# Second attention of a four-layer block: one list of four units per engine, and probability transposes in 64-row half tiles

## The chip, the cores and the metric

One core of a Trainium2 chip. The metric is device time in microseconds (us) of one execution, the median of the runs shown. In this text PE is TensorE, DVE VectorE, ACT ScalarE, POOL GpSimd and SP SyncE. PEld is PE's weight load, which may run beside its matmuls.

## The reference

All in f32, on x of 8 x 512 tokens of width 128; four layers, each behind a layer norm and added to x:

```
x = x + L0_attn(ln(x))     # 16 heads of 8, two softmaxes, difference with a learned lambda
x = x + L0_ffn(ln(x))      # 8 experts, top 2, capacity 1280, rows sorted into lists
x = x + L1_attn(ln(x))     # the change is here
x = x + L1_ffn(ln(x))      # 8 experts, top 4, and a shared expert

# L1_attn, b = 8 batches, 16 heads of 64, 512 tokens
K, Q, V = einsum('bpd,ihd->biph', x, W_K / W_Q / W_V)
scores  = einsum('biph,biqh->biqp', K, Q), causal mask
attn    = softmax(scores / 8)
z       = einsum('biph,biqp->biqh', V, attn)
out     = einsum('bqf,df->bqd', z as (b, q, 1024), W_O)
```

## The kernel before

Five instruction streams, one for each engine, are written by hand from one list, `schedule()`, and meet at semaphores (`Signal`). Every engine executes its own stream strictly in that order.

The second attention works on pairs of heads: 8 batches x 8 head pairs. A head pair has four *units*, one for each block of 128 query rows, in the order qb = 3, 0, 2, 1. A unit's scores are 128 x 128(qb+1), since the mask cuts the rest, so the four units have 512, 128, 384 and 256 columns. For a unit `u`:

- `scores1` (PE, L1391): two matmuls, one for each head of the pair, in the two 64-row tiles of the array (the head width is 64).
- `soft` (DVE, L2257): mask, scale and row maximum of each head, out of the PSUM pair `pS`.
- `exp1` (ACT, L1651): exp with the sum, for each head.
- `norm`: reciprocal (DVE, L2266) and multiplication (POOL, L2535).
- `turnp` (PE, L1404): transposes of the probabilities, 128 x 128 blocks, full array, head 0 into `tbank[0]`, head 1 into `tbank[1]`. ACT copies head 0 out (L1661), DVE head 1 (L2273).
- `values` (PE, L1424): once for a head pair, V times the transposed probabilities, both heads in two 64-column tiles, into `bank[2]`; ACT copies it out (L1669).

Beside them stand `heads` (H0 the queries, L1376 into `misc`, copied out by DVE, L2248; H1 the keys, L1372 into `bank[2]`, copied out by ACT, L1641), the value projection of the next batch (`v1`, L1361, into `misc` from the second batch on), the output projection once a batch (`op1`, L1433), transposes of the normed rows (L1165), router logits (L1269) and the combine of the expert rows (POOL fetches, DVE L2223, L2226). `misc` is one PSUM bank with many users; each waits until the one before has been copied out (`misc_free`).

The order of the second attention is the table `ROUND`. A round is two units, and a table row has two strings for each engine: rounds with an even and with an odd number. A token is a piece: S scores, M soft, X exp, N norm, T transposes (unit, head), H heads, V values, C a piece of the combine, A and B work of other stages, I the first value projections. `-1` says: of the round before. I call two rounds, four units, a *round pair*.

## Time and profile before

| | |
|---|---|
| median of 3 runs | 1513.7 us (1513.47 to 1518.37) |
| profiled execution, its own time | 1500.44 us |
| its span, first to last instruction | 1499.2 us |
| PE busy | 1437.6 us (96%) |
| DVE busy | 1074.6 us (72%) |
| ACT busy | 951.5 us (63%) |
| POOL busy | 745.5 us (50%) |
| mean granted clock of PE | 0.994 |

Busy time is what the profiler sees of an engine's instructions. A busy PE is not PE at its peak: drains and loads between matmuls are inside it, since the recorded ends of matmuls overlap. The profiled execution is one of its own, 13 us under the median of the timed runs.

### The profile page before, as it was taken

The page shows a single profiled execution, that of the slowest core. Times are in us where ns is not written, and L with a number is a line of the kernel's source. Part 1 is how long each engine was busy: PE and PEld are TensorE (multiplying, and loading weights), DVE is VectorE, ACT ScalarE, POOL GpSimd, SP SyncE. Part 2 cuts the span into 40 slices and gives each one's busy share as a digit, 9 for nine tenths or more (in the row PEclk, how much of TensorE's full clock was granted, in tenths as well). Part 3 has the DMA queues.
Part 4 walks back from the last instruction along what each step waited for, and adds up shares of the span by engine and source line. Part 5 has one row for each costly group of instructions (what it writes and reads, how often), then busy time and mean ns, then how long its engine had stood idle before and what let it go on. Part 6 is the DMA issues. An engine that isn't in the chain of part 4 may idle for free.

```text
span 1499.2 us, 26266 instructions
## 1 busy us (share of the span) xinstructions
PE 1437.6 (96%) x8801; PEld 856.5 (57%) x8801; DVE 1074.6 (72%) x3430; ACT 951.5 (63%) x2448; POOL 745.5 (50%) x1260
## 2 busy tenths in 40 slices
PE   4999999999989999979999999999999999998999
PEld 2434443444438889855565655656565565655666
DVE  5899999999944777547677687777767777674333
ACT  4588888887884334436767677676767777673221
POOL 7334656665455633633636365454636444353322
PEclk9999999999999999989999999999999999999999
DMA  7266655556334665720000000000000000020421
GB/s 142 57 159 134 143 141 148 110 106 150 113 131 165 213 211 190 256 64 1 15 1 15 1 12 5 3 14 1 16 2 14 3 1 2 2 58 1 99 76 52
DMA packets 70600, 113.39 MB, mean 76 GB/s; under 512 B 18857, under 2 KB 35114, under 8 KB 70458
## 3 DMA queue, kind: packets, MB, share of 16 engines
q0 software_dynamic: 33104, 61.73, 16.9%
q1 hardware_dynamic: 36928, 49.19, 10.9%
q8 instruction: 71, 1.16, 0.3%
q10 hardware_dynamic: 434, 0.79, 0.2%
q14 instruction: 63, 0.52, 0.1%
HBM read 71.86 MB, written 39.91 MB: 75 GB/s over the span
## 4 chain that ended last, share of the span: by engine, by line
PE 79%; DVE 10%; ACT 6%; issue 2%; POOL 1%; DMA 1%; SPq 0%; ACTq 0%; DVEq 0%; POOLq 0%
PE pS L1391 10%; PE bank L1424 9%; PE bank L1404 8%; PE bank L1235 6%; PE pS L1206 4%; PE bank L1433 4%; PE pS L1310 4%; PE bank L1376 4%; PE bank L1324 4%; PE bank L1361 4%; PE pS L1311 4%; PE bank L1372 3%; DVE mx L1831 3%; ACT ar L1561 3%; PE bank L1472 3%; PE bank L1226 2%
## 5 line engine op out<-in xcount | busy, mean ns | idle before, releaser
L2535 POOL TENSOR_SCALAR ar<-ar,rd 128x512 f32<-128x512 f32 (+3 forms) x512 | 269.3, 540 | 325.9 <-DVE rd L2266 324.0
L1831 DVE TENSOR_REDUCE mx<-pS 128x1 f32<-128x512 f32 x512 | 326.3, 677 | 19.4 <-PE pS L1206 17.6
L1651 ACT ACTIVATE ar<-ar,nm 128x512 f32<-128x512 f32 (+3 forms) x512 | 285.9, 560 | 83.1 <-DVE nm L2257 82.4
L2257 DVE CUSTOM_DVE_ANT_0 ar<-pS,maskf 128x512 f32<-128x512 f32 (+3 forms) x512 | 227.3, 481 | 6.3 <-PE pS L1391 4.4
L1561 ACT ACTIVATE ar<-bank 128x512 f32<-128x512 f32 x342 | 194.1, 598 | 44.8 <-PE bank L1226 41.6
L1404 PE MATMUL bank<-identr,all_r 128*128 128x128 f32 x1280 | 211.4, 287 | 4.6 <-DVE ar L2273 2.5
L1206 PE MATMUL pS<-all_r 64*128 64x512 f32 x512 | 205.7, 477 | 5.6 <-DVE mx L1831 4.7
L1404 PEld LDWEIGHTS bank<-identr,all_r 128*128 128x128 f32 x1280 | 134.3, 140 | 108.1 <-issue 83.4
L1661 ACT COPY ar<-bank 128x512 f32<-128x512 f32 (+3 forms) x256 | 107.4, 419 | 110.3 <-PE bank L1404 108.2
L1391 PE MATMUL pS<-ar 64*128 64x512 f32 (+3 forms) x1024 | 172.9, 456 | 0.8 <-DVE ar L2248 0.8
L1206 PEld LDWEIGHTS pS<-all_r 64*128 64x128 f32 x512 | 85.3, 192 | 127.7 <-DVE mx L1831 110.3
L2273 DVE COPY ar<-bank 128x512 f32<-128x512 f32 (+3 forms) x256 | 124.0, 484 | 40.9 <-PE bank L1404 39.8
L1424 PE MATMUL bank<-ar 128*64 128x512 f32 (+3 forms) x1024 | 152.0, 439 | 0.6 <-ACT ar L1661 0.6
L1226 PE MATMUL bank<-all_r 64*128 64x512 f32 x342 | 142.9, 458 | 1.8 <-ACT ar L1561 1.3
L1235 PE MATMUL bank<-ar 128*32 128x512 f32 x1024 | 139.8, 608 | 0.0
L1391 PEld LDWEIGHTS pS<-ar 64*128 64x128 f32 x1024 | 88.0, 186 | 68.8 <-issue 42.3
L1561 ACT ACTIVATE ar<-pS 128x512 f32<-128x512 f32 x170 | 101.6, 598 | 19.5 <-PE pS L1226 18.1
L2120 DVE TENSOR_TENSOR ar<-pS,ar 128x256 f32<-128x256 f32 (+1 forms) x156 | 59.2, 396 | 73.8 <-ACT ar L1600 73.5
L1424 PEld LDWEIGHTS bank<-ar 128*64 128x64 f32 x1024 | 67.9, 136 | 73.8 <-issue 59.1
L1600 ACT ACTIVATE ar<-pS 128x256 f32<-128x256 f32 (+1 forms) x156 | 56.8, 365 | 68.2 <-PE pS L1311 67.6
L1651 ACT ACTIVATION_READ_ACCUMULATOR ar<-ar,nm 128x1 f32 x512 | 97.0, 190 | 0.0
L2436 POOL DMA_DIRECT2D all_r<-dm x64 | 39.9, 627 | 95.0 <-DMA dm<-xT 90.1
(306 smaller groups left out, 2638.2 us busy)
## 6 DMA issues: line engine op xcount, KB each, us to landing
rows_in<-zrow SPq DMA_DIRECT2D x16, 1024.0 KB, 5.3
ar<-gd SPq DMA_DIRECT2D x16, 512.0 KB, 6.7
all_r<-dk POOLq DMA_DIRECT2D x56, 128.0 KB, 3.7
dk<-xT SPq DMA_DIRECT2D x21, 256.0 KB, 3.6
dq<-xT SPq DMA_DIRECT2D x16, 256.0 KB, 5.0
rows_out<-ar SPq DMA_DIRECT2D x32, 128.0 KB
all_r<-dq POOLq DMA_DIRECT2D x28, 144.0 KB, 3.8
all_r<-dq POOLq DMA_DIRECT2D x28, 128.0 KB, 3.4
```

The lines of the kernel that those rows point to most:

```text
L1206: M.matmul(bS[n % 3], qst[b % 2][rows, i, 128 * qb:128 * qb + 128], kst[b % 2][rows, i, :], start=True, stop=True).then_inc(*s_sc.inc(Gr, c))
L1226: M.matmul(bST[n % 3], kst[b % 2][rows, i, 128 * kb:128 * kb + 128], qst[b % 2][rows, i, :], start=True, stop=True).then_inc(*s_st.inc(Gr, ...
L1235: M.matmul(bO[32 * j:32 * j + 32, :], vst[b % 2][:, kb, 4 * g + j, :], pt[s_pv.no[Gr, kb, j] % NPT], start=(kb == 0), stop=(kb == 3)).then ...
L1391: M.matmul(pS[s][:, 512 * a:512 * a + w], yT[i][0][head, 128 * qb:128 * qb + 128], yT[i][1][head, 0:w], start=True, stop=True).then_inc(*s ...
L1404: ins = M.transpose(tbank[a][:, at_:at_ + 128].bitcast(F32R), pr_r[pi][:, 128 * t:128 * t + 128], identr[:, :])
L1424: ins = M.matmul(bank[2][64 * a:64 * a + 64, 128 * kb:512], v1[b % 2][:, kb, 64 * h:64 * h + 64], w, start=(kb == 0), stop=(kb == 3))
L1561: S.activation(pt[n % NPT], bST[n % 3], ACT.Exp, scale=QK_SCALE).then_inc(*s_ex.inc(Gr, kb, j))
L1651: S.activation(p, p, ACT.Exp, bias=nm1[:, c:c + 1], scale=-1.0, accum_out=den1[:, c:c + 1]).then_inc(*s_e1.inc(u, a))
L1831: V.tensor_reduce(mx[Gr % 2][:, col:col + 1], bS[n % 3], AX.X, ALU.max, negate=True).then_inc(*s_mx.inc(Gr, c))
L2257: V.tensor_tensor_reduce(pr_[pi][:, 0:w], pS[u % 2][:, 512 * a:512 * a + w], maskf[:, 512 - w:512], -0.125, 3e38, ALU.add, ALU.min, accum_ ...
L2273: V.tensor_copy(pT4[i][:, 3 - qb:4, w:w + 128], tbank[1][:, 0:w].rearrange("p (t n) -> p t n", n=128)).then_inc(*s_td.inc(u, 1))
L2535: G.tensor_scalar(p, p, rd1[:, c + a:c + a + 1], 1.0, ALU.mult, ALU.mult).then_inc(*s_p1.inc(u, a))
```

## The change

The rounds of two units become one list of four units for each engine (`PAIR`), whose loop runs over head pairs `z`. The keys `B0`/`B1` and `A0`/`A1` are what stood in the two rounds' B and A, C0 to C3 their four C. In the values' token V-1 the number now counts head pairs.

A unit's transposes become one piece for both heads (PE does all at `T`, and nothing at the token's second half). Each 128 x 128 block is turned as two halves: rows 0 to 63 and rows 64 to 127 of the probabilities, each with the 64 x 64 part of the identity, in the two 64-row tiles, half 0 into `tbank[0]` and half 1 into `tbank[1]`. So a transposed half has 128 partitions and 64 columns. ACT copies half 0 of both heads, in two instructions, DVE half 1. The wait is for both heads' probabilities and for both copies of the unit before.

```diff
-ROUND = {
-    "PE": ("S0 S1 T00-1 H0 T01-1 H1 I B T10-1 T11-1",
-          "S0 S1 T00-1 T01-1 V-2 T11-1 T10-1 I B"),
...
+PAIR = {
+    "PE": "S0 S1 T2-1 H0 H1 I B0 T3-1 S2 S3 T0 V-1 B1 T1",
+    "DVE": "M0 C0 N3-1 T21-1 H0 C1 H1 N0 M1 I B0 T31-1 A0 N1 M2 T01 C2 M3 N2 A1 C3 T11 B1",
...
+    for z in range(NU // 4 + 2):
...
+        pieces = {"I": taken(first_v1) if z == 0 else []}
         for n in range(2):
+            pieces["B%d" % n] = taken(beside_round, 2 * (z % 8) + n, b) if now else []
+            pieces["A%d" % n] = taken(after_round, 2 * (z % 8) + n, b) if now else []
+        for n in range(4):
             pieces["C%d" % n] = taken(next, back, None) if now else []
...
+    def turned_half(u, head, half):
+
+        qb, i = UNITS[u][2], (u // 4) % 2
+        n, w = 64 * (qb + 1), 128 * (qb + 1) + 64 * half
+        of_ = tbank[half][:, 256 * head:256 * head + n].rearrange("p (t n) -> p t n", n=64)
+        if head:
+            return pT4[i][:, 3 - qb:4, w:w + 64], of_
+        rows = pT[i][:, 128 * qb:128 * qb + 512 * (qb + 1)].rearrange("p (t n) -> p t n", n=512)
+        return rows[:, :, 64 * half:64 * half + 64], of_
...
         def turnp(u, a):
+
+            if a:
+                return
             qb = UNITS[u][2]
-            pi = (2 * u + a) % NP
-            PE.wait_ge(*s_p1.at(u, a))
+            PE.wait_ge(*s_p1.at(u, 1))
             if u:
-                PE.wait_ge(*(s_td if a else s_ta).at(u - 1, a))
-            else:
-                PE.wait_ge(*s_eo.at(NP_ - 2 + a))
+                PE.wait_ge(*s_ta.at(u - 1, 0))
+                PE.wait_ge(*s_td.at(u - 1, 1))
+            else:
+                PE.wait_ge(*s_eo.at(NP_ - 1))
             for t in range(qb + 1):
-                at_ = 128 * (qb - t if a else t)
-                ins = M.transpose(tbank[a][:, at_:at_ + 128].bitcast(F32R), pr_r[pi][:, 128 * t:128 * t + 128],
-                                  identr[:, :])
-            ins.then_inc(*s_t1.inc(u, a))
+                for head in range(2):
+                    to = 256 * head + 64 * (qb - t if head else t)
+                    for half in range(2):
+                        rows = slice(64 * half, 64 * half + 64)
+                        ins = M.transpose(tbank[half][:, to:to + 64].bitcast(F32R),
+                                          pr_r[(2 * u + head) % NP][rows, 128 * t:128 * t + 128], identr[rows, rows])
+                        if t == qb and head:
+                            ins.then_inc(*s_t1.inc(u, half))
...
-            V.tensor_copy(pT4[i][:, 3 - qb:4, w:w + 128],
-                          tbank[1][:, 0:w].rearrange("p (t n) -> p t n", n=128)).then_inc(*s_td.inc(u, 1))
+            for head in range(2):
+                to, of_ = turned_half(u, head, 1)
+                ins = V.tensor_copy(to, of_)
+            ins.then_inc(*s_td.inc(u, 1))
```

ACT's copy changes as DVE's does. Three places of the order show what moves.

PE, from the scores of units 0 and 1 of a head pair, before: transposes (L1404) of the head pair before stand ahead of, between and behind the queries (L1376) and keys (L1372).

```order
L1404 MATMUL bank<-identr,all_r 128x128 x2
L1361 MATMUL bank<-wv,xnT 128x512
L1391 MATMUL pS<-ar 128x512 x2
L1391 MATMUL pS<-ar 128x128 x2
L1404 MATMUL bank<-identr,all_r 128x128 x3
L1376 MATMUL bank<-xnT,res 128x512
L1404 MATMUL bank<-identr,all_r 128x128 x3
L1372 MATMUL bank<-xnT,att 128x512
L1361 MATMUL bank<-wv,xnT 128x512
L1404 MATMUL bank<-identr,all_r 128x128 x4
L1391 MATMUL pS<-ar 128x384 x2
L1391 MATMUL pS<-ar 128x256 x2
```

The same place in the changed kernel, where the scores are L1393, the transposes L1412, the queries L1378, the keys L1374 and the value projection L1363:

```order
L1271 MATMUL bank<-rt,xT 128x8 x4
L1412 MATMUL bank<-identr,all_r 128x64 x4
L1393 MATMUL pS<-ar 128x512 x2
L1393 MATMUL pS<-ar 128x128 x2
L1412 MATMUL bank<-identr,all_r 128x64 x12
L1378 MATMUL bank<-xnT,oT 128x512
L1374 MATMUL bank<-xnT,att 128x512
L1363 MATMUL bank<-wv,xnT 128x512
L1412 MATMUL bank<-identr,all_r 128x64 x8
L1393 MATMUL pS<-ar 128x384 x2
L1393 MATMUL pS<-ar 128x256 x2
```

All transposes of a unit stand together, next to scores, and queries, keys and value projection follow each other. The x12 are 6 couples of halves.

PE, around the values (L1424, after the change L1433), before, in a round pair whose second B is a value projection:

```order
L1404 MATMUL bank<-identr,all_r 128x128 x8
L1424 MATMUL bank<-ar 64x512 x2
L1424 MATMUL bank<-ar 64x384 x2
L1424 MATMUL bank<-ar 64x256 x2
L1424 MATMUL bank<-ar 64x128 x2
L1404 MATMUL bank<-identr,all_r 128x128 x2
L1361 MATMUL bank<-wv,xnT 128x512
```

and after:

```order
L1412 MATMUL bank<-identr,all_r 128x64 x16
L1433 MATMUL bank<-ar 64x512 x2
L1433 MATMUL bank<-ar 64x384 x2
L1433 MATMUL bank<-ar 64x256 x2
L1433 MATMUL bank<-ar 64x128 x2
L1363 MATMUL bank<-wv,xnT 128x512
L1412 MATMUL bank<-identr,all_r 128x64 x4
```

The value projection moved ahead of unit 1's transposes, which now stand directly before the next scores.

DVE, where the next batch's norm is applied (L1772, after the change L1781), before: the reciprocal, the norm, the copy of unit 1's transposes, then the soft pieces (L2257) of the next scores, the queries' copy (L2248) and unit 2's transposes' copy (L2273):

```order
L2266 RECIPROCAL rd<-den 128x2
L1772 TENSOR_SCALAR xn<-x,ln_mv,ln_rs 128x128 x4
L2273 COPY ar<-bank 128x128
L2266 RECIPROCAL rd<-den 128x2
L2257 ISA ar,nm<-pS,maskf 128x512
L2257 ISA nm 128x1
L2257 ISA ar,nm<-pS,maskf 128x512
L2257 ISA nm 128x1
L2248 COPY ar<-bank 128x512
L2273 COPY ar<-bank 128x3x128
```

and after (soft is L2266, the copies of the transposes L2283, the queries' copy L2257):

```order
L2275 RECIPROCAL rd<-den 128x2
L1781 TENSOR_SCALAR xn<-x,ln_mv,ln_rs 128x128 x4
L2283 COPY ar<-bank 128x64 x2
L2266 ISA ar,nm<-pS,maskf 128x512
L2266 ISA nm 128x1
L2266 ISA ar,nm<-pS,maskf 128x512
L2266 ISA nm 128x1
L2275 RECIPROCAL rd<-den 128x2
L2283 COPY ar<-bank 128x3x64 x2
L2257 COPY ar<-bank 128x512
```

Unit 2's copies moved ahead of the queries' copy; unit 1's copy still stands behind the norm.

## Rows read from the trace of the kernel before

**Rows 1.** The page: part 1, busy time by engine.
```profile
PE 1437.6 (96%) x8801; PEld 856.5 (57%) x8801; DVE 1074.6 (72%) x3430; ACT 951.5 (63%) x2448; POOL 745.5 (50%) x1260
```

**Rows 2.** The scores' line L1391: duration in ns, first and last start in us.
```profile
L1391 PE MATMUL pS<-ar x1024: 269/481/693, 658.0 to 1344.7; 64*128 64x512 f32 x43, 64*128 64x128 f32 x43, 64*128 64x256 f32 x43, 64*128 64x384 f32 x42
```

**Rows 3.** One batch: stretch, its length, busy time of PE, PEld, DVE, ACT, POOL, clock.
```profile
852.51:938.39 85.88, 85.66 (x548) 51.73 (x547) 63.80 (x258) 60.59 (x184) 45.40 (x80) 1.00 0.03 8
```

**Rows 4.** Chain of waits through one round pair: start us, us, what.
```profile
904.11 1.28 PE pS L1391 x8
905.39 0.38 PE bank L1404 x3
905.77 0.93 PE bank L1376 x2
906.70 0.21 PE bank L1404 x3
...
907.84 0.86 PE bank L1361 x2
908.70 0.29 PE bank L1404 x4
...
910.27 0.81 PE bank L1404 x8
911.07 2.31 PE bank L1424 x16
913.38 0.30 PE bank L1404 x2
```

**Rows 5.** PE's weight loads: start us, us, what; x8 is first start to last end.
```profile
906.11 0.14 PEld L1404 LDWEIGHTS bank<-identr,all_r 128*128 128x128 f32 x1 [0.24 <-POOL ar L2535]
...
910.20 0.73 PEld L1404 LDWEIGHTS bank<-identr,all_r 128*128 128x128 f32 x8 [0.33 <-issue]
```

**Rows 6.** Timeline at a 32-column transpose of the first attention.
```profile
216.02 0.10 PEld L1214 LDWEIGHTS bank<-identr,mp 128*32 128x32 f32 x1 [0.37 <-issue]
216.02 0.24 PE L1214 MATMUL bank<-identr,mp 128*32 128x128 f32 x1
...
216.06 0.30 PEld L1278 LDWEIGHTS bank<-rr,ustrict 128*128 128x128 f32 x2
```

**Rows 7.** Timeline at the queries of a round pair.
```profile
905.61 1.09 PE L1376 MATMUL bank<-xnT,oT 128*128 128x512 f32 x2
...
906.74 0.69 DVE L2248 COPY ar<-bank 128x512 f32<-128x512 f32 x1 [0.23 <-PE bank L1376]
...
907.48 0.39 PEld L1361 LDWEIGHTS bank<-wv,xnT 128*128 128x128 f32 x2 [0.47 <-DVE ar L2248]
```

**Rows 8.** Waits in the second attention: us in total, times, longest.
```profile
PEld bank L1361 <- DVE ar L2248: 19.9, 42, 0.5
```

**Rows 9.** Timeline where the next batch's norm is applied.
```profile
864.36 1.67 DVE L1772 TENSOR_SCALAR xn<-x,ln_mv,ln_rs 128x128 f32<-128x128 f32 x4
...
864.57 1.35 PE L1391 MATMUL pS<-ar 64*128 64x512 f32 x8
...
865.95 0.28 DVE L2273 COPY ar<-bank 128x128 f32<-128x128 f32 x1
```

**Rows 10.** Copies of the transposes: shape, count, busy us, mean ns.
```profile
L2273 DVE COPY ar<-bank 128x512 f32<-128x512 f32 x63 | 43.3, 687 | 1.9 <-PE bank L1404 1.8
...
L1661 ACT COPY ar<-bank 128x512 f32<-128x512 f32 x63 | 35.6, 565 | 0.0
...
L2273 DVE COPY ar<-bank 128x128 f32<-128x128 f32 x63 | 17.8, 283 | 18.9 <-PE bank L1404 18.4
L1661 ACT COPY ar<-bank 128x128 f32<-128x128 f32 x63 | 16.8, 266 | 25.3 <-PE bank L1404 24.8
```

**Rows 11.** DVE at the start of the second attention.
```profile
665.81 0.35 DVE L2223 SCALAR_TENSOR_TENSOR x<-ar,kw,x 128x128 f32<-128x128 f32 x1 [7.86 <-DMA ar<-rows_out,idx]
```

**Rows 12.** Chain of waits at the output projection: start us, us, what.
```profile
852.51 7.16 PE bank L1433 x64
```

More of the change, by code:

```diff
@@ L591, in schedule, with part @@
     back = returned(1)
-    def part(token, x, pieces):
+    def part(token, z, pieces):
         name, late = token.split("-") if "-" in token else (token, "0")
-        y = x - int(late)
+        y = z - int(late)
         kind, n = name[0], name[1:]
-        if kind in "CAI":
+        if kind in "ABCI":
             return pieces[name]
-        if kind in "BV":
-            z = (y - 1) // 2
-            if kind == "B":
-                return pieces["B"]
-            return [("values", (z, kb)) for kb in range(4)] if y % 2 and 0 <= z < NU // 4 else []
-        if not 0 <= y < NU // 2:
+        if not 0 <= y < NU // 4:
@@ L606, in part @@
             return []
-        u = 2 * y
+        u = 4 * y
+        if kind == "V":
+            return [("values", (y, kb)) for kb in range(4)]
         if kind == "H":
-            r = 8 * (y // 16) + y % 16 // 2 + 1
-            return [("heads", (r // 8, r % 8, int(n)))] if y % 2 == 0 and r < 8 * NB else []
-        if kind == "S":
-            return [("scores1", (u + int(n),))]
-        if kind == "M":
-            return [("soft", (u + int(n),))]
-        if kind == "N":
-            return [("norm", (u + int(n),))]
@@ L617, in part @@
-        return [({"X": "exp1", "T": "turnp"}[kind], (u + int(n[0]), int(n[1])))]
-    def first_v1(x):
-        for t in (2 * x, 2 * x + 1):
+            r = y + 1
+            return [("heads", (r // 8, r % 8, int(n)))] if r < 8 * NB else []
+        if kind == "T":
+            return [("turnp", (u + int(n[0]), int(n[1:] or 0)))]
+        if kind == "X":
+            return [("exp1", (u + int(n[0]), int(n[1])))]
+        return [({"S": "scores1", "M": "soft", "N": "norm"}[kind], (u + int(n),))]
@@ L621, in first_v1 @@
+    def first_v1():
+        for t in range(4):
             add("v1", 0, t, 0)
             add("v1", 0, t, 1)
-    for x in range(NU // 2 + 5):
-        b, k = x // 16, x % 16
-        now = x < NU // 2
-        if now and k == 8 and b + 2 < NB:
+    for z in range(NU // 4 + 2):
+        b = z // 8
+        now = z < NU // 4
+        if now and z % 8 == 4 and b + 2 < NB:
             back = returned(b + 2)
-        pieces = {"I": taken(first_v1, x) if x < 2 else [], "B": taken(beside_round, k, b) if now else []}
+        pieces = {"I": taken(first_v1) if z == 0 else []}
@@ L630, in schedule @@
         for n in range(2):
+            pieces["B%d" % n] = taken(beside_round, 2 * (z % 8) + n, b) if now else []
+            pieces["A%d" % n] = taken(after_round, 2 * (z % 8) + n, b) if now else []
+        for n in range(4):
             pieces["C%d" % n] = taken(next, back, None) if now else []
-        pieces["A"] = taken(after_round, k, b) if now else []
-        for engine, rounds in ROUND.items():
-            for token in rounds[x % 2].split():
-                for unit in part(token, x, pieces):
+        for engine, tokens in PAIR.items():
+            for token in tokens.split():
+                for unit in part(token, z, pieces):
@@ L928, in program @@
     s_p1 = Signal(nc, "probs1", [(u, a) for (u,) in of("norm") for a in range(2)])
-    s_t1 = Signal(nc, "probs_turned", of("turnp"))
+    s_t1 = Signal(nc, "probs_turned", s_s1.marks)
     s_ta = Signal(nc, "turned_by_act", [k for k in of("turnp") if k[1] == 0])
@@ L1656, in turnp @@
                 return
-            qb, i, w = UNITS[u][2], (u // 4) % 2, 128 * (UNITS[u][2] + 1)
             ACTE.wait_ge(*s_t1.at(u, 0))
-            o = pT[i][:, 128 * qb:128 * qb + 512 * (qb + 1)].rearrange("p (t n) -> p t n", n=512)
-            S.copy(o[:, :, 0:128],
-                   tbank[0][:, 0:w].rearrange("p (t n) -> p t n", n=128)).then_inc(*s_ta.inc(u, 0))
+            for head in range(2):
+                to, of_ = turned_half(u, head, 0)
+                ins = S.copy(to, of_)
+            ins.then_inc(*s_ta.inc(u, 0))
         def values(pair, kb):
@@ L2270, in turnp @@
                 return
-            qb, i, w = UNITS[u][2], (u // 4) % 2, 128 * (UNITS[u][2] + 1)
             DVE.wait_ge(*s_t1.at(u, 1))
-            V.tensor_copy(pT4[i][:, 3 - qb:4, w:w + 128],
-                          tbank[1][:, 0:w].rearrange("p (t n) -> p t n", n=128)).then_inc(*s_td.inc(u, 1))
+            for head in range(2):
+                to, of_ = turned_half(u, head, 1)
+                ins = V.tensor_copy(to, of_)
+            ins.then_inc(*s_td.inc(u, 1))
         def op1(b):
```

11 rows, old and new, of tables (PAIR, ROUND) are left out of this document.

## Prediction

> **What bounds the kernel now.** I read four views in this order. The page's first part [rows 1] says that PE is busy for 96% of the span, DVE for 72% and ACT for 63%, so the question is what the change does to PE's list. The second attention runs from the first L1391 matmul at 658.0 us to about 1355 us [rows 2]. The busy time in one batch of it, 85.88 us from one output projection to the next [rows 3], is 85.66 us for PE at full clock, 63.80 for DVE and 60.59 for ACT. The reader is to see that PE has no idle time to give here: only work or switches taken from PE shorten it. The chain of waits of one round pair [rows 4] confirms it, since every piece is PE's, one after another, with no wait between them. Eight batches of such pairs make the stretch.
>
> That chain prices every piece, because PE is in order (of pieces that come twice one row stands: the keys and a second value projection read 0.93 like the queries, the second scores 1.28). From [rows 4], in us: scores of two units 1.28; 3 transposes behind scores 0.38; queries (L1376) behind transposes 0.93; 3 transposes behind a projection 0.21; keys 0.93; a value projection (L1361) behind another projection 0.86; 4 transposes 0.29; scores 1.28; 8 transposes 0.81; values 2.31; 2 transposes 0.30. The sum is 9.58 us, and a second value projection adds 0.93.
>
> Three prices follow.
> - A transpose: (0.81 - 0.38)/5 = 0.086 us. The load row agrees: 8 loads in 0.73 us, one alone 0.14 long, so (0.73 - 0.14)/7 = 0.084 apart [rows 5].
> - A change of tile shape. A 512-column projection takes 0.86, so 640 columns of scores should take 1.07 and took 1.28: 0.21. Scores to transposes costs 0.38 - 0.21 = 0.17. The 1280 columns of values should take 2.15 and took 2.31: 0.16. Behind values, 2 transposes took 0.30 instead of 0.13: 0.17. So each change costs 0.16 to 0.21 us, the drain and a weight load that nothing hides.
> - A full-width f32 load behind a short matmul: 0.93 - 0.86 = 0.07.
>
> The Trainium skill (TensorEngine Tiling (Array Packing), Key Properties) says the same of the first part, that changing the tiling mode drains the engine; by that, the trace agrees.
>
> **The change, part by part.** Per round pair (four units) PE's list goes from six changes of shape to four (scores and transposes now share the 64-row shape), or five where a piece stands in B1, between values and the last transposes.
>
> *Transposes.* 20 full ones become 20 couples, two 64-row halves side by side. The moving operand halves to 64 columns, the stationary one keeps 128. What matters is whether the load or the matmul sets the 0.085. A load of 32 columns (L1214) is followed by the next instruction's load 0.04 later, although the matmul between them also moves 128 columns [rows 6]. So the pace follows the loaded columns and does not wait for a 128-column matmul. I take 0.085 a couple: no gain from the halves. That two row tiles load and stream side by side is shown by the scores: 8 matmuls, two heads in two row tiles, fit into the 1.28 that one head's columns explain. Bounds: 0.06 a couple if the pace was the matmul's, 0.17 if the tiles take turns.
>
> *The round pair without waits.* Scores behind a same-shape transpose 1.07 + 0.10 = 1.17; 6 couples 0.21 + 3 x 0.085 = 0.46, less 0.03 for the shorter last matmul; queries behind a change 1.06; keys 0.86; value projection 0.86; 4 couples behind a change 0.44; scores 1.17; 8 couples 0.61; values 2.31; 2 couples behind a change 0.27. Sum 9.18: 0.40 less. With a piece in B1 (six of eight pairs in a batch) a fifth change costs about 0.13 of that: 0.25 less. Per batch: 2 x 0.40 + 6 x 0.25 = 2.3 us.
>
> *A new wait behind the queries' copy.* Before, 3 transposes (0.21) stood between queries and keys. Now queries, keys and the piece in B0 follow each other, and the piece in B0 needs the same bank as the queries, emptied by DVE (L2248). In [rows 7] the queries' last matmul is recorded to end at 906.70, the copy runs from 906.74 to 907.43, PE's load starts at 907.48, and 0.10 of it is exposed: 1.05 after the queries leave the array at about 906.53. The keys cover 0.86, so at least 0.19 is bare. DVE also has the two score reductions, a reciprocal and now two transpose copies ahead of that copy, which makes it about 0.13 later. I take 0.32 for each of the seven pairs in eight whose B0 is filled: 2.2 us a batch. The list before paid next to nothing for it: the whole stretch has 19.9 us of "load waits for L2248", hidden behind the matmul then running [rows 8].
>
> *Coupled transposes wait for both copies.* Each unit's transposes now need both engines' copies of the unit before and both heads' probabilities. Where the next batch's norm is applied (L1772, 1.67 us on DVE [rows 9]), DVE's copy of the one-column-block unit ends 1.66 after the scores start (864.57 to 866.23). PE wants the next transposes at 1.08, so it stands 0.6 to 1.0: I take 0.8 a batch.
>
> *Copies.* 256 copies on each of ACT and DVE become 512 of half the width. From 266 to 565 ns on ACT and 283 to 687 on DVE over 128 to 512 columns [rows 10], a copy has a fixed part of 0.165 and 0.148 us. Extra per batch: 32 x 0.165 = 5.3 us on ACT (77% busy) and 4.7 on DVE (80%). Neighbours on DVE overlap by about 0.08 [rows 7], so what later work feels is about 0.07 a unit. It is hidden by PE's own time except where PE waits for the copy, which the two waits above include. If that cover is gone, it is 0.3 us a pair, 18 us in all.
>
> *The rest.* DVE's first reduction now stands ahead of the first combine, which waits 7.86 us for a DMA [rows 11]. The queries' copy still stands behind that combine, so this gives back 1 us at most. SP's list only renames its rounds, and POOL's tensor_scalars keep their number.
>
> Sum: 8 x (-2.3 + 2.2 + 0.8) = +5.6, less about 1 at the start: **+5 us**. The profiled execution took 1500.4 us (span 1499.2), the median of the three runs shown is 1513.7. I add the 5 us to the median: 1519. About 0.3% (4.5 us) is what this measurement can tell from no change.
>
> **The rivals.**
> - *The pace falls with the moving columns* (0.06 a couple). 20 x 0.025 x 64 = 32 us leave PE's work, but DVE and ACT, then at 82% and more, and the waits for copies give back about half: 5 - 15 = -10 us, 1504. The sign turns at 0.077 a couple. For it: the matmul and the load are both 128 wide in every L1404 row, so those rows can't tell them apart. Against it: [rows 6]. The Trainium skill (TensorE: Matmul & The Clock Gate, Part 3) has a rule that leads here, that a load overlaps running matmuls only when the row group differs; the value projection's load of 907.48, all rows, starts while the keys' matmuls still run, until about 907.84 [rows 4, 7], which speaks against it.
> - *Two row tiles are slower than one full array for this operation*: loads at the f32 pace (0.112 for 128 columns, 7.16 us for 64 [rows 12]), or tiles that take turns. At 0.11: 20 x 0.025 x 64 = +32, of which the new waits swallow about 15, so 5 + 17 = +22, 1536. The Trainium skill (TensorE: Matmul & The Clock Gate, LDWEIGHTS) gives 128/1.2 = 107 ns for any load of 128 columns; the L1404 loads here are 84 apart. At 0.17: 20 x 0.085 x 64 = +109, less some 30 of waits that it hides, 1593. For it: no transpose in a 64-row tile is in the trace. Against it: the scores run side by side.
> - *The copies become the path*: DVE's and ACT's lists slip, PE waits the 0.3 us a pair above on top: +5 + 15, 1534. For it: coupled releases, 80% busy in order. Against it: DVE still waits for PE, 0.23 ahead of the queries' copy [rows 7].
> - *Nothing shows*: the waits are 0.1 a pair smaller than walked and changes of shape are worth their full 0.2: within 4 us of before.
>
> **How the numbers follow.** Forecast (pace near 0.085, waits as walked, -1 to +11 us): 50%, of which about two fifths stay under 4.5. Moving columns: 18%, plus 3% for smaller waits that end faster too. Slower tiles: 12%, two thirds of it near +22. Copies: 12%. Nothing shows: 5%. Faster by over 0.3%: 0.21. Within: 0.2 from the forecast, 0.05, and 0.05 of the middle between rivals: 0.3. Slower: 0.49. The range from 1504 (first rival) to 1536 (0.11 a couple, or copies) leaves out the serial tiles and the far end of the first rival, some 15 to 20%.
>
> **What the changed profile would show.** Scores next to transposes with no gap, four couples' loads 0.085 apart, and a round pair of about 9.5 us without and 10.5 with a piece in B1. A new group of waits on PE, for DVE's queries' copy, of about 0.3 each some 50 times, and one for transposes after the norm's application. ACT and DVE near 77% and 80% a batch. The forecast is wrong if the couples' loads are not 0.08 to 0.09 apart, if PE's waits for copies come to less than 1.5 us or more than 5 us a batch, or if the scores behind transposes still cost 1.28.

## The result, and the profile after

The changed kernel takes 1521.3 us (median of 12 runs), the kernel before 1513.65 beside it (12 runs): ratio 1.0046, 95% interval 1.0025 to 1.0068. Two disturbed runs of the changed kernel are left out of the ratio. On another chip it was compared once more (below): 1.0033, 1.0005 to 1.0061. So it is slower by 5 to 7 us; the forecast was +5.

Batches are numbered from 0 here, and so are a batch's eight round pairs where they carry a number. "PE stands" means idle time of PE in the chain of waits.

The page of the changed kernel, part 1, for [rows 1]:

```profile
PE 1437.8 (95%) x10081; PEld 851.7 (56%) x10081; DVE 1082.6 (71%) x3686; ACT 962.5 (64%) x2704; POOL 745.0 (49%) x1260
```

PE's busy time has not moved (1437.6 before), DVE gained 8.0 us and ACT 11.0. The span of this execution, 1514.6 us, is not to be set against the 1499.2 of before: the first L1393 scores start at 667.2 us, 9.2 later than in [rows 2], although the program up to there is the same, and every execution profiled on one of the three chips used below has this lag (664.9 to 669.6), those on the other two have not (658.0 to 660.5). Which chips the first comparison and the profile of before ran on is not known. By the lag, the changed kernel's first profile is from the third chip and that of before is not; that would also explain why the profile of before (1500.44 us) lies 13 us under its timed median, since the kernel before has medians of 1502.35, 1503.03 and 1512.92 us on the three chips. So I compare stretches.

Two batches of the changed kernel, in the columns of [rows 3], batch 3 and batch 6 (the second window begins one pair into it):

```profile
934.69:1022.16 87.47, 85.34 (x710) 50.83 (x709) 64.95 (x288) 62.16 (x216) 45.30 (x81) 1.00 0.03 8
1206.47:1292.75 86.28, 85.33 (x711) 50.88 (x709) 62.75 (x282) 61.87 (x218) 37.42 (x73) 1.00 0.01 2
```

Before, each batch takes 85.88 us. Batch 6 here takes 86.28, batch 3 takes 87.47, with PE busy for 85.3 us in both, 0.3 less than before. PE's idle time grew from 0.2 us to 0.95 and 2.1. The two do not separate work from waiting: a matmul that waits for its weights is recorded longer, so the waits behind the keys below are inside the busy time.

The chain of waits of a round pair, for [rows 4], here one with a value projection in B1:

```profile
924.34 1.18 PE pS L1393 x8
925.52 0.43 PE bank L1412 x12
925.95 1.05 PE bank L1378 x2
927.01 0.86 PE bank L1374 x2
927.86 0.03 issue
927.89 1.12 PE bank L1363 x2
929.02 0.44 PE bank L1412 x8
929.46 1.18 PE pS L1393 x8
930.64 0.59 PE bank L1412 x16
931.23 2.30 PE bank L1433 x16
933.53 1.06 PE bank L1363 x2
934.59 0.27 PE bank L1412 x4
```

The reader is to see the forecast pieces: scores behind transposes 1.18 (1.17 forecast), 6 couples behind them 0.43, queries behind a change of shape 1.05, keys 0.86, 4 couples 0.44, 8 couples 0.59, values 2.30, 2 couples 0.27. From 6 to 8 couples is 0.16 us (0.59 less 0.43), so 0.08 a couple, the pace of before. All of these are within 0.03 of the forecast. Only the value projection behind the keys is long: 0.03 and 1.12 in place of 0.86.

Why it is long is in the timeline at the queries, for [rows 7]:

```profile
936.40 1.13 PE L1378 MATMUL bank<-xnT,res 128*128 128x512 f32 x2
...
937.15 0.60 DVE L2283 COPY ar<-bank 128x192 f32<-128x192 f32 x2
...
937.67 0.68 DVE L2257 COPY ar<-bank 128x512 f32<-128x512 f32 x1
...
938.41 0.30 PEld L1363 LDWEIGHTS bank<-wv,xnT 128*128 128x128 f32 x2 [0.86 <-DVE ar L2257]
```

DVE's copy of the queries (L2257) follows the copy of unit 2's transposes (L2283) without a gap, and PE's load for the value projection follows the queries' copy. The load's idle time of 0.86 is mostly covered by the keys' matmuls; what PE itself waits is 1.15 - 0.86 = 0.29 us (0.32 forecast).

Where the next batch's norm is applied, for [rows 9]:

```profile
872.40 1.35 PE L1393 MATMUL pS<-ar 64*128 64x512 f32 x8
872.46 1.69 DVE L1781 TENSOR_SCALAR xn<-x,ln_mv,ln_rs 128x128 f32<-128x128 f32 x4
...
874.07 0.34 DVE L2283 COPY ar<-bank 128x64 f32<-128x64 f32 x2
...
874.56 0.67 PE L1412 MATMUL bank<-identr,all_r 64*128 64x64 f32 x12 [0.81 <-DVE ar L2283]
```

PE could start the transposes of unit 2 at 873.5, 1.1 behind its scores, and does at 874.56, behind DVE's norm and the copy of unit 1: 1.06 us a batch (0.8 forecast).

The copies of the transposes by shape, for [rows 10] (count, busy us, mean ns):

```profile
L2283 DVE COPY ar<-bank 128x256 f32<-128x256 f32 x128 | 48.0, 417 | 0.8 <-PE bank L1412 0.8
...
L1670 ACT COPY ar<-bank 128x256 f32<-128x256 f32 x128 | 41.4, 375 | 56.4 <-PE bank L1412 56.4
...
L2283 DVE COPY ar<-bank 128x64 f32<-128x64 f32 x128 | 22.3, 215 | 32.6 <-PE bank L1412 32.2
...
L1670 ACT COPY ar<-bank 128x64 f32<-128x64 f32 x128 | 20.8, 214 | 37.6 <-PE bank L1412 37.1
```

Two half copies are busy 0.75 us on DVE (48.0/64) where one whole took 0.69, and 0.35 where it took 0.28: 0.06 more, not the fixed part of 0.148, because neighbours on an engine overlap.

**What the forecast did not have.** In one or two round pairs of each of five batches the wait behind the keys is 0.5 to 0.85 us longer. The timeline of pair 6 of batch 2:

```profile
913.95 0.68 PE L1412 MATMUL bank<-identr,all_r 64*128 64x64 f32 x12
...
915.93 0.62 DVE L2283 COPY ar<-bank 128x192 f32<-128x192 f32 x2 [0.53 <-PE bank L1412]
...
917.38 1.13 PE L1363 MATMUL bank<-wv,xnT 128*128 128x512 f32 x2 [0.83 <-DVE ar L2257]
```

The transposes of unit 2 run at 913.95. Their semaphore counts up at 915.87, 1.24 us after the end that the record gives, where outside these pairs it is 0.01 after it. (This pair is in batch 2; batch 3 has the same in its pairs 5 and 6.) DVE stands 0.53 us for it, copies, copies the queries, and PE stands 0.83. In batch 3 that makes 87.47 out of 86.28.

### The profile page after: what moved, and what is told of

Read it like the earlier page. It is cut to its first block, busy times and chain, and to the rows that moved or that the text cites. A ratio compares the mean times of both kernels' runs of the same rounds, so it can differ in the third digit from the quotient of the medians.

```text
span 1514.6 us, 29146 instructions
## 1 busy us (share of the span) xinstructions
PE 1437.8 (95%) x10081; PEld 851.7 (56%) x10081; DVE 1082.6 (71%) x3686; ACT 962.5 (64%) x2704; POOL 745.0 (49%) x1260
## 4 chain that ended last, share of the span: by engine, by line
PE 76%; DVE 12%; ACT 6%; issue 3%; POOL 2%; DMA 1%; ACTq 0%; DVEq 0%; POOLq 0%
PE pS L1393 8%; PE bank L1433 8%; PE bank L1412 7%; PE bank L1237 6%; PE bank L1363 4%; PE bank L1378 4%; PE pS L1208 4%; PE bank L1442 4%; DVE mx L1840 4%; PE pS L1312 3%; PE pS L1313 3%; PE bank L1326 3%; PE bank L1481 3%; PE bank L1374 3%; PE bank L1228 3%
## 5 line engine op out<-in xcount | busy, mean ns | idle before, releaser
L2266 DVE CUSTOM_DVE_ANT_0 ar<-pS,maskf 128x512 f32<-128x512 f32 (+3 forms) x512 | 227.6, 482 | 16.8 <-PE pS L1393 16.0
L1670 ACT COPY ar<-bank 128x256 f32<-128x256 f32 (+3 forms) x512 | 122.8, 292 | 152.1 <-PE bank L1412 151.5
L2283 DVE COPY ar<-bank 128x256 f32<-128x256 f32 (+3 forms) x512 | 140.1, 315 | 75.4 <-PE bank L1412 75.1
L1412 PEld LDWEIGHTS bank<-identr,all_r 64*128 64x128 f32 x2560 | 128.7, 137 | 81.2 <-POOL ar L2545 68.1
L1393 PE MATMUL pS<-ar 64*128 64x512 f32 (+3 forms) x1024 | 173.2, 457 | 0.8 <-DVE ar L2257 0.8
L1412 PE MATMUL bank<-identr,all_r 64*128 64x64 f32 x2560 | 157.4, 252 | 12.2 <-DVE ar L2283 7.2
L1433 PE MATMUL bank<-ar 128*64 128x512 f32 (+3 forms) x1024 | 152.5, 440 | 0.7 <-ACT ar L1670 0.7
L1393 PEld LDWEIGHTS pS<-ar 64*128 64x128 f32 x1024 | 87.7, 186 | 49.9 <-issue 31.2
L1433 PEld LDWEIGHTS bank<-ar 128*64 128x64 f32 x1024 | 68.2, 137 | 72.3 <-issue 59.4
```

The costliest lines, as they stand in the source:

```text
L1393: M.matmul(pS[s][:, 512 * a:512 * a + w], yT[i][0][head, 128 * qb:128 * qb + 128], yT[i][1][head, 0:w], start=True, stop=True).then_inc(*s ...
L1412: ins = M.transpose(tbank[half][:, to:to + 64].bitcast(F32R), pr_r[(2 * u + head) % NP][rows, 128 * t:128 * t + 128], identr[rows, rows])
L1433: ins = M.matmul(bank[2][64 * a:64 * a + 64, 128 * kb:512], v1[b % 2][:, kb, 64 * h:64 * h + 64], w, start=(kb == 0), stop=(kb == 3))
L2266: V.tensor_tensor_reduce(pr_[pi][:, 0:w], pS[u % 2][:, 512 * a:512 * a + w], maskf[:, 512 - w:512], -0.125, 3e38, ALU.add, ALU.min, accum_ ...
L2283: ins = V.tensor_copy(to, of_)
```

## The experiments

All times are ratios to the kernel before on the same chip, with the 95% interval. "A batch" is the length of batch 3, from its first scores to the next batch's. Three chips were used: e1 to e4 ran on one, e5 to e8 on a second, e9 to e12 on a third. The changed kernel itself was timed on the second (e8) and, by its lag, on the third, not on the first.

| run | ratio | interval | a batch, us |
|---|---|---|---|
| kernel before | 1 | | 85.9 |
| changed kernel | 1.0046 | 1.0025 to 1.0068 | 87.5 |
| e1 fetches apart | 0.9993 | 0.9967 to 1.0019 | 86.3 |
| e2 norm one pair later | 1.0143 | 1.0108 to 1.0177 | 91.2 |
| e3 queries' copy first | 1.0025 | 0.9997 to 1.0054 | 86.2 |
| e4 order alone | 1.0034 | 1.0009 to 1.0058 | 87.1 |
| e5 norm in the gap | 0.9976 | 0.9951 to 1.0001 | 85.5 |
| e6 e5 and e3 | 0.9972 | 0.9948 to 0.9997 | 85.2 |
| e7 e6, whole transposes | 1.0067 | 1.0044 to 1.0090 | 87.2 |
| e8 changed kernel again | 1.0033 | 1.0005 to 1.0061 | 86.3 |
| e9 ACT's copy early | 1.0057 | 1.0035 to 1.0079 | 87.6 |
| e10 filler in the last pair | 1.0036 | 1.0021 to 1.0050 | 87.5 |
| e11 e5, e9, e10 | 1.0012 | 0.9998 to 1.0027 | 86.8 |
| e12 e5, e10 | 1.0000 | 0.9981 to 1.0019 | 86.6 |

### The late signals: e1 and e8

```diff
-    "POOL": "N3-1 N0 C0 N1 A0 C1 N2 A1 C2 C3",
+    "POOL": "N3-1 C3 N0 C0 N1 A0 C1 N2 A1 C2",
```

> POOL's two row fetches that stand side by side behind the norm of unit 2 (C2 C3) are taken apart: C3 now stands behind the norm of unit 3. In the changed kernel the unit 2 transposes of two pairs in a batch (the sixth and seventh, batches with fetches alone) have their end signalled 1.1 to 1.2 us late, and PE then waits 0.5 and 0.75 us more behind the keys. Theory A, the late signal belongs to the fetches that run at that moment: the two waits go, about 1.25 us in each of five batches, -6 us against the changed kernel (ratio to before 1.0005 in place of 1.0046). Theory B, it belongs to the router pieces of these pairs, or to the half transposes as such: the late signals stay where they are and the time with them, 0. If the signal is late wherever a fetch meets a transpose, it may also move to another place: then between 0 and -6.

The late signals were gone and a batch took 86.3. That looked like theory A. The changed kernel itself, run again on the second chip, takes the conclusion away:

> The changed kernel itself once more, beside the others on this chip. If the late end signals of the transposes in the sixth and seventh pair belong to the program, they are there again, in the same five batches, and the batch takes 87.4 us; if they were an accident of one profiled execution, the batch takes 86.3. The ratio to before should be 1.003 to 1.006.

The same place, transposes of unit 2, their copy and the value projection behind the keys, in e8:

```profile
901.13 0.68 PE L1412 MATMUL bank<-identr,all_r 64*128 64x64 f32 x12
...
902.50 0.60 DVE L2283 COPY ar<-bank 128x192 f32<-128x192 f32 x2
...
903.75 0.30 PEld L1363 LDWEIGHTS bank<-wv,xnT 128*128 128x128 f32 x2 [0.85 <-DVE ar L2257]
```

The copy follows with nothing to wait for, although the fetches (POOL L2535) stand where they stood. Its batch:

```profile
1016.79:1103.06 86.27, 85.33 (x710) 50.90 (x708) 64.61 (x289) 61.90 (x218) 45.03 (x80) 1.00 0.03 8
```

So the late signals do not belong to the program alone, nor are they an accident of one execution, as they come back below. Neither of the two first chips showed one in any of eight profiles of seven different edits and the changed kernel; the third chip showed them in all four of its profiles, e9 to e12, and the changed kernel's first profile has them, with the 9 us lag of that chip. On that chip they stand in the six batches that have fetches (0 to 5) and in neither of the two that have none (batch 6 above, at 86.28, and the last). That the fetches take part is thus likely; that separating them helps was not shown, since e1 did not run there. Whether the kernel before has late signals there is open too. They cost the changed kernel about 1.2 us in four batches and 0.5 in one, some 5 us of that profile, but its ratio is only 0.0013 higher than e8's, inside the intervals. Nor is e1's 0.9993 a gain over e8's 1.0033: the intervals overlap, the chips differ, and the batches of both profiles are equally long to 0.1 us (86.33 and 86.27).

### The order alone: e4

```diff
             for t in range(qb + 1):
                 for head in range(2):
...
+                    ins = M.transpose(tbank[head][:, at_:at_ + 128].bitcast(F32R),
+                                      pr_r[(2 * u + head) % NP][:, 128 * t:128 * t + 128], identr[:, :])
...
```

Each engine's copy of a unit is one instruction again, as before.

> The new order of all engines, with both heads' transposes together, but the transposes as before: full array, 128 x 128, one copy for each engine. This separates the order from the half tiles. My theory: the half tiles save the changes of shape between scores and transposes, 0.40 us in a pair without and 0.25 in one with a piece in B1, 2.3 us a batch; without them the new order has before's changes and the new waits (queries' copy, norm, late signals), so +18 us against the changed kernel, about +25 against before, less some 3 us for waits that the longer list hides: ratio 1.013 to 1.017. Rival: half tiles bring nothing net because two copies per engine in place of one cost what the shapes save: then this kernel takes the time of the changed one, ratio about 1.005.

The theory's 1.013 to 1.017 failed: 1.0034, the time of the changed kernel (1.0033 on another chip), as its rival had it. But this batch is not the changed kernel's:

```profile
1011.93:1099.06 87.13, 86.83 (x547) 51.55 (x545) 63.44 (x256) 60.73 (x184) 45.03 (x81) 1.00 0.03 7
```

87.13 us: the order alone costs 1.25 a batch over before, and the half tiles then give back 0.85, not 2.3. PE has 86.83 us of work here, 1.5 more than with half tiles, but the longer list also covers waits: the value projection behind the keys takes 1.05 in place of 1.15, since one copy of unit 2 on DVE is 0.53 long and two are 0.60, and at the norm PE stands 0.36 us instead of 1.06. (Of the 1.5 us, the waits behind the keys count as busy in both.) Behind the output projection DVE has an unbroken list of 6.4 to 6.6 us up to the copy of unit 1, which PE must wait for; what PE saves in that pair it only waits longer. That the timed ratio is no higher in spite of the longer batches has a counterpart behind the stretch: e4's profile takes 159.7 us from the last pair's scores to its end, e8's 166.9 (below).

### The norm: e2 and e5

e2 moves the application one pair later, and with it all of A0, ahead of the copy of unit 3.

```diff
-        if k == 3 and b + 1 < NB:
+        if k == 4 and b + 1 < NB:
             add("apply", "c", b + 1)
-    "DVE": "... M1 I B0 T31-1 A0 N1 M2 ...",
+    "DVE": "... M1 I B0 A0 T31-1 N1 M2 ...",
```

> DVE applies the next batch's norm (1.69 us) one pair later and in another place of its list: ahead of the copy of unit 3's transposes, where it stands idle for 1.2 us, in place of ahead of unit 1's copy. My theory, that coupled transposes wait for the norm's application: PE's wait of 1.06 us behind the scores goes in seven batches, -7.4 us against the changed kernel, ratio about 0.9997. Rival: the work is only moved and DVE's list is what counts; then unit 3's copy, about 0.5 later, makes the transposes of unit 0 wait instead, and the gain is under 3 us.

It was 1.4% slower, so the rival held. The copy of unit 3 and the transposes of unit 0 in one of the three pairs that grew:

```profile
871.49 0.48 DVE L2283 COPY ar<-bank 128x128 f32<-128x128 f32 x2
...
872.12 1.03 PE L1412 MATMUL bank<-identr,all_r 64*128 64x64 f32 x16 [1.67 <-DVE ar L2283]
```

DVE's idle time ahead of that copy is not slack: PE wants unit 0's transposes right behind the next scores. They wait 1.67 us here, and the statistics and the router's pieces, which moved along, cost two more pairs 1.06 and 0.92. The wait is the same, 1.66 to 1.68 us, in batches 2 to 6, but what follows is not: in three of them (2, 3, 5) PE then has 3.4 us at the lower clock level and the pair is 2.7 us longer than in e8, in the other two (4, 6) the clock stays and the pair is 1.1 longer. The batch of 91.2 us in the table is one of the three; batches 4 and 6 take 89.5 and 89.4. The moved work must go where both DVE and what follows it wait for something long. That is the output projection:

```diff
-        if k == 2 and b + 1 < NB:
+        if k == 2 and b == 0:
             add("ln", "c", b + 1)
-        if k == 3 and b + 1 < NB:
+        if k == 3 and b == 0:
             add("apply", "c", b + 1)
...
+    def next_norm(b):
+        add("ln", "c", b + 1)
+        add("apply", "c", b + 1)
...
+        pieces["L"] = taken(next_norm, b) if z % 8 == 1 and 0 < b < NB - 1 else []
-    "DVE": "... N0 M1 I B0 T31-1 ...",
+    "DVE": "... N0 M1 I L B0 T31-1 ...",
-    "POOL": "N3-1 N0 C0 ...",
+    "POOL": "N3-1 N0 L C0 ...",
```

> The next batch's norm (statistics, root, application; 1.2 us and 1.7 us on DVE) moves to where DVE stands idle for 7.0 us behind the output projection, ahead of that wait, in the six batches that have an output projection. Nothing else changes against the changed kernel. My theory, DVE's unbroken list from the output projection to the copy of unit 1's transposes (6.6 us) is what PE waits for in the next scores: the wait of 1.06 us goes, 6 x 1.06 = -6 us against the changed kernel, and the six pairs from the output projection on read about 8.9 us in place of 9.9. Rival, drawn from the last run in which this norm was moved and cost 3 us or more a batch: any move of it delays a copy that PE needs; then not faster.

DVE around the output projection in e5, statistics, application and the addition of the projection:

```profile
851.90 0.87 DVE L1736 BATCH_NORM_STATS2 ln_st<-x 128x6 f32<-128x128 f32 x4
...
854.67 1.12 DVE L1786 TENSOR_SCALAR xn<-x,ln_mv,ln_rs 128x128 f32<-128x128 f32 x4 [1.49 <-POOL ln_rs L2391]
...
859.01 0.69 DVE L2294 TENSOR_TENSOR x<-bank,x 128x512 f32<-128x512 f32 x1 [3.22 <-PE bank L1447]
```

All of it lies ahead of the 3.22 us that DVE still waits. The batch is 85.48 us, 0.8 less than e8's, and the pair behind the projection 9.09 in place of 9.9 (8.9 was expected). The ratio is 0.9976, beside e8's 1.0033 on the same chip, where the intervals still overlap. The third chip has a second pair of kernels that differ in this move alone, e12 and e10 below: 1.0000 (up to 1.0019) against 1.0036 (from 1.0021), 0.36% or 5.4 us, where 6 were expected. These intervals do not overlap, so the norm's move is a gain that the timed runs show.

```profile
1009.22:1094.70 85.48, 85.08 (x709) 50.94 (x708) 64.24 (x288) 61.71 (x216) 44.99 (x81) 1.00 0.03 8
```

### The queries' copy: e3, e6 and e7

```diff
-    "DVE": "M0 C0 N3-1 T21-1 H0 C1 ...",
+    "DVE": "M0 C0 N3-1 H0 T21-1 C1 ...",
```

> DVE copies the queries ahead of unit 2's transposes. My theory: PE's wait behind the keys is the copy's own latency plus 0.10 us for which DVE is held by the other copy. The wait falls from 0.25-0.30 to 0.15-0.20, and in the two pairs with a late signal DVE no longer stands in front of it, so 7 x 0.10 + up to 0.5 = 0.7 to 1.2 us a batch, -6 to -9 us. Rival: DVE then stands idle for about 0.4 us ahead of the queries' copy in each pair, its list slips by as much, and unit 0's or unit 1's exponentials or copies come late: 0 or slower.

Each pair with a queries' wait became 0.10 us shorter (9.36 for 9.46, 10.41 for 10.51), as forecast, but a batch stayed at 86.2: in the pair behind the norm unit 2's copy came late for unit 3 (+0.5), and in the last batch, which has no value projections, five of the seven pairs lost 0.3 to 0.65 in this way (71.8 for 70.1 us over all seven). So theory and rival each held in their place.

> The norm in the gap and, on DVE, the queries' copy ahead of unit 2's transposes. If the waits are what ate the gain of the half tiles, a batch takes 86.25 (queries first) less 1.05 (norm) less 0.5 (the third pair, where unit 2's late copy held up unit 3) = 84.7 us against 85.87 before: 6 to 7 batches x 1.2 = -8 us against before, ratio 0.994 to 0.996. Rival, the two moves disturb each other as DVE is 80% busy: ratio 0.998 or more.

```profile
1009.38:1094.56 85.18, 84.63 (x710) 50.83 (x709) 65.09 (x288) 62.05 (x216) 45.01 (x81) 1.00 0.03 8
```

85.18 us, 0.7 under before, ratio 0.9972: the lowest ratio measured, but 0.0004 from e5, so no gain over it is shown. The forecast of the batch was 84.7, too low by 0.5, of which the pair behind the norm's old place kept 0.3 (9.38 for e5's 9.09); the last batch is 1.7 longer than e5's (71.8 for 70.1), as in e3.

> The same two moves with the transposes as before (full array, 128 x 128, one copy for each engine). It prices the half tiles with the waits largely gone. My theory: half tiles save 0.40 us in a pair without and 0.25 in a pair with a piece in B1, 2.3 us a batch, of which the first comparison showed only 0.84 because waits took the rest; here 1.6 to 2.3 us a batch show, this kernel is 13 to 18 us slower than the one with half tiles. Rival: the extra copies cost as much wherever they stand, and the difference stays at 0.84 a batch, 7 us.

```profile
1017.28:1104.53 87.25, 86.77 (x547) 51.53 (x545) 63.90 (x256) 61.29 (x184) 45.02 (x81) 1.00 0.03 7
```

With whole transposes the same two moves bring nothing (87.25 after 87.13). Against e6 this is 2.07 us a batch, and 0.95% = 14 us of the kernel: here the half tiles show what they save, inside both ranges of the theory. The chain of a pair of e7, beside that of the changed kernel above:

```profile
1006.74 1.28 PE pS L1396 x8
1008.02 0.64 PE bank L1413 x6
1008.66 0.93 PE bank L1381 x2
1009.59 0.86 PE bank L1377 x2
1010.45 1.05 PE bank L1366 x2
1011.50 0.29 PE bank L1413 x4
```

Scores 1.28 for 1.18, six transposes 0.64 for 0.43, the queries behind them 0.93 for 1.05.

### The end of the stretch: e9 to e12

In e8's profile the stretch from the first scores to the last pair's is 4 us shorter than before (678.1 and 682.0), and yet its span is 4.0 longer. In these two profiles the loss is behind it. The windows from the last pair's scores to the end of its values, of before, of the changed kernel, and of e8 (the seventh number, behind the five busy times, is the granted clock):

```profile
1340.04:1353.89 13.85, 11.39 (x79) 6.68 (x78) 7.20 (x29) 8.56 (x27) 6.79 (x16) 1.00 0.23 49
```

```profile
1353.41:1369.31 15.90, 11.62 (x113) 7.49 (x111) 7.97 (x37) 9.09 (x34) 7.04 (x16) 0.89 0.28 60
```

```profile
1336.28:1355.93 19.65, 15.37 (x112) 8.94 (x110) 8.06 (x37) 9.08 (x34) 7.00 (x16) 0.68 0.23 47
```

The granted clock was 1.00, 0.89 and 0.68: in the third, 13.6 of 19.65 us ran at the lower level, 1.2 GHz. Ahead of the fall stands this, PE in e8:

```profile
1337.38 0.67 PE L1412 MATMUL bank<-identr,all_r 64*128 64x64 f32 x12
...
1340.21 0.69 PE L1412 MATMUL bank<-identr,all_r 64*128 64x64 f32 x8 [2.16 <-ACT ar L1670]
...
1340.68 2.53 PE L1393 MATMUL pS<-ar 64*128 64x384 f32 x8
```

and in before:

```profile
1341.32 0.71 PE L1404 MATMUL bank<-identr,all_r 128*128 128x128 f32 x6
...
1342.49 0.36 PE L1404 MATMUL bank<-identr,all_r 128*128 128x128 f32 x2 [0.46 <-POOL ar L2535]
...
1343.13 0.33 PE L1404 MATMUL bank<-identr,all_r 128*128 128x128 f32 x2 [0.27 <-DVE ar L2273]
```

The last pair has no queries or keys for PE to do. Before, its transposes waited 0.46 and 0.27 us. Coupled, they stand 2.16 us for ACT's copy of unit 2, and then the scores take 2.53 us for 1.34. Ten profiles have the new order and no filler. Nine of them have such intervals, 3.4 to 13.6 us in sum, the first beginning 3.5 to 5.4 us behind the start of these scores; e4 and the kernel before have none. In the seven that have the half tiles and ACT's list of the changed kernel the wait is 2.15 to 2.16 us. A shorter wait does not decide it: e4 also waits here, 1.90 us, and nothing follows, while e7 waits 1.88 and 3.4 us at the lower level follow; e2's waits of 1.67 above go both ways as well. (The Trainium skill, TensorE: Matmul & The Clock Gate, Part 1, ties the granted clock to how busy PE has been; by that, the traces agree in that a fall stands behind a wait each time, but they do not show why a wait of 1.7 to 1.9 us was followed by one in some cases and not in others.)

```diff
-    "ACT": "X00 A0 X01 T20-1 H1 ...",
+    "ACT": "X00 A0 T20-1 X01 H1 ...",
```

> ACT copies unit 2's transposes ahead of the second head's exponential of unit 0, nothing else changes against the changed kernel. In the last pair PE has no queries and keys to do and stood 2.16 us in one piece for this copy, and in the last batch (no value projections) about 0.3 us a pair; in the other batches the copy is not waited for. Theory A, these waits and the lower granted clock that follows them are what the changed kernel loses behind the stretch: the last batch falls from 70.1 to about 68.5 us, the idle piece from 2.16 to about 0.7, no or one interval at half clock follows it, together -3 to -6 us against the changed kernel, ratio 0.999 to 1.001. Theory B, the clock falls there whatever PE waits for: only the waits go, -2 us, ratio 1.002. It is slower if unit 0's probabilities come late by the 0.5 us.

Theory A's times failed: 1.0057, no faster than the changed kernel. But the edit did not remove the idle piece, so it does not decide between the theories. PE still stood 1.86 us, now for POOL's norm of unit 3; 6.8 and then 3.4 us at the lower level followed; and four of the seven pairs of the last batch became 0.2 longer (70.9 for 70.1 us over all seven), as unit 0's probabilities came late.

```diff
+            for _ in range({NU - 6: 2, NU - 2: 1}.get(u, 0)):
+                M.matmul(misc[:, :], wqk[0][:, 0:128], xnT[(NB - 1) % 2][:, :], start=True, stop=True)
```

> Three 128 x 512 matmuls whose result nobody reads (into the bank of the queries, which is free then) fill PE's waits in the last pair of the second attention: two behind unit 2's transposes, where PE stood 2.16 us, one where it stood 0.9. Nothing else changes against the changed kernel; the work is extra. Theory A, the clock is granted lower there because PE stands idle: the intervals at half clock just behind the last scores (3.4 us in one profile, 13.6 in another) go, -2 to -6 us, ratio about 1.000. Theory B, the clock falls whatever PE does there: nothing gained, ratio 1.0035 to 1.005 as the changed kernel.

```profile
1356.02:1370.70 14.68, 13.00 (x118) 7.59 (x116) 7.87 (x37) 9.17 (x34) 7.06 (x16) 1.00 0.30 64
```

The clock stayed at 1.00 and the window shrank to 14.68 us, although PE does more. In all three profiles with filler (e10 to e12) no interval at the lower level follows within 30 us of the last scores, and from those scores to the end it takes 159.9 to 161.4 us, against 161.1 to 166.9 in the nine with such an interval and 159.1 and 159.7 in before and e4. So for the clock theory A holds in the profiles: the clock stays in three of three with filler and falls in both without it that carry the third chip's lag. Its time, -2 to -6 us, is not shown: the timed ratio is 1.0036 beside 1.0046, each inside the other's interval.

> The norm in the gap and the filler, with ACT's list as changed: the difference to the kernel with the early copy prices that copy; the difference to the norm alone (0.9976) prices the filler. Theory A: 0.995 to 0.996. Theory B: 0.9975.

> The norm in the gap behind the output projection, ACT's copy early, and the filler. Theory A adds up: the norm alone gave 0.9976, the clock and the waits of the last batch 3 to 6 us more: 0.994 to 0.996, the best of all. If the early copy or the filler brings nothing: 0.9975.

1.0000 and 1.0012, so the forecasts of 0.994 to 0.996 failed. Both have the third chip's late signals, some 5 us (0.3%), so they can't be set against e5's 0.9976 from another chip. On their own chip, e12 against e10 prices the norm's move (above). Between the two the early copy costs 0.0012, within the intervals.

## Why the prediction was right

- **Sum and sign.** +5 us forecast, +7 and +5 measured: right in the pieces of a steady batch, and in the sum by luck. The sum took eight equal batches of +0.7 and a start of -1. Where no signal is late, batches 1 to 6 are +0.3 to +0.4 each (86.27 against 85.87), the last one, which has no value projections and no next norm, is -1.4 (70.1 against 71.5 over seven pairs), and the first about -2 (below). That makes some -1 us where +5 was forecast. In the profiles the rest comes from two things that the prediction did not name: late signals, some 5 us in the changed kernel's first profile, and the end of the stretch, 2.0 us in that profile and 7.8 in e8's (from the last pair's scores to the end: 159.1 us before, 161.2 and 166.9 after).
- **Pace of the couples.** Right: 0.08 was measured where 0.085 was taken, 0.06 and 0.11 or more were the rivals'. Both rivals are excluded by it.
- **Changes of shape, -2.3 a batch.** Right. A pair with a piece in B1 takes 10.51 us with 0.29 of waiting, so 10.22 without, against 10.49 before: 0.27 (0.25 forecast). A pair without takes 9.46, so 9.17, against 9.56: 0.39 (0.40 forecast). e6 against e7 shows 2.07 a batch in all, extra copies included.
- **The queries' copy, +2.2.** Right in mechanism, 0.24 to 0.29 in six pairs and 0.19 at the output projection (7.35 for 7.16): 1.9. e3 and e4 showed that 0.10 of the 0.29 is DVE's two copies of unit 2, which end later than one (0.60 for 0.53), the rest the copy's own latency.
- **The norm, +0.8.** 1.06 in batches 1 to 6, none in the last. The prediction took it for a copy behind 1.7 us of norm; e4 and e5 show that it is DVE's whole list from the output projection on, so that it grows by whatever PE saves in that pair.
- **Copies.** Mis-sized: +5.3 and +4.7 us busy a batch were forecast from the fixed part of a copy, the profile's first part has +11.0 and +8.0 for all eight batches, 1.4 and 1.0 each. So ACT is busy for 72% of a batch and DVE for 75%, not the 77% and 80% that were to show. The 0.07 that "later work feels" was nearly right (0.06); it was read from an overlap of 0.08 that [rows 7] do not show, but the copies after the change do (2 x 0.417 less 0.75 on DVE).
- **The start, -1.** The first eight pairs took 95.4 us before and 90.6 (e8) and 93.3 (changed kernel) after. These include 13.7, 6.8 and 13.7 us at the lower clock level. The profiles with half tiles and 13.7 us of it (the changed kernel, e5, e9, e10, e11) read 93.3 to 93.6, so at an equal clock about 2 us are saved; how much of them is DVE's order stays open, and there is one profile of before.
- **A slip.** The time given for tiles that take turns, 1593, leaves out the +5 that its neighbour has: it should read 1598. Nothing rests on it.
- **What was missed.** First, the last pair: coupled transposes turn a wait of 0.7 into one of 2.16 us, and the granted clock falls behind it. In e8's profile this window is 5.8 us longer than before, and more than the whole difference of the spans. The timed runs are in keeping with this, no more: on the second chip, 21 of 35 executions of the kernel before had a mean clock of 0.992 or 0.994, 12 at 0.994 (about 1501.3 us) and 9 at 0.992 (1503.2); of twelve executions of the changed kernel one was at 0.994 with 1501.15 us, three at 0.991 with 1504.4 to 1505.4, two at 0.989 with 1507.8 and 1508.0, and six lower, up to 1517.4. So the one execution at the same clock took the same time, and the others had lower clocks; which stretch had the lower clock in them is not known. That a fall stands behind the idle piece, and none where filler takes its place, is shown in the profiles; a timed gain from it is not. Second, the late signals of one chip, whose cause is open.

## What to carry to other kernels

Where the engine that bounds the kernel gets shorter work, look in each repeated stretch for the place at which another engine's unbroken list is already as long: there the saving turns into waiting, and here more than half of it did (0.85 of 2.1 us a batch were left) until DVE's norm went into its 7 us gap and its copies were put in another order. A sum for one batch times the number of batches is right only for the batches that are alike: here the first and the last went the other way. Idle time ahead of an instruction is slack only if nobody waits right behind it. When pieces of work are coupled, check the last iteration, where the work that covered the coupling is missing.

## What the runs showed of the hardware

- Two 64-row tiles turn a 128 x 128 block as two halves in 0.08 us, a full-array transpose of the block takes 0.084 to 0.086. Scores behind transposes in the same 64-row shape take 1.18 us, behind full-array ones 1.28 (e7).
- On one of three chips a PE semaphore counted up 0.8 to 1.5 us after the matmul started that carried it (0.26 normally), while PE itself ran on, in the same pairs of the same batches in all five profiles of the half tiles there and in none of the eight of the new order on the other two. Whether the kernel before has it there was not profiled.
- In the last pair a wait of 2.15 to 2.16 us, behind 12 us in which PE had run almost without a break, was followed by 3.4 to 13.6 us at the lower clock level in seven of seven profiles. Waits of 1.86 to 1.90 there were followed by it in e7 and e9 and not in e4, equal waits of 1.67 in e2 in three batches and not in two, and waits of 0.46 and 0.27 in the kernel before were not.
